# Local-attention rounds: residual and gates moved ahead of the recurrence's parts on VectorE, outputs turned in another PSUM bank

## The reference

```python
xn = _layernorm(x, axis=-1)
s = _L1_attn_ref(xn, ...)         # gated delta rule, 16 heads of 8, 256 steps in order
g = _silu(_L1_ffn_ref(xn, ...))   # two layers of local attention and a gated MLP
x = x + s * g
```

```python
S = S * jnp.exp(gt)[..., None, None]
pred = jnp.einsum('bhk,bhkv->bhv', kt, S)
dv = (vt - pred) * bt[..., None]
S = S + jnp.einsum('bhk,bhv->bhkv', kt, dv)
ot = jnp.einsum('bhk,bhkv->bhv', qt, S)
```

```python
h = shift_token(x)
q, k, v = split(h @ wqkv)
q, k = rotary_xpos(l2norm(q) * qs, l2norm(k) * ksc)
x = x + local_attention(q, k, v) @ wo
h = layernorm(shift_token(x)) * lg + lb
a, g = split(h @ w1 + b1)
x = x + (a * gelu(g)) @ w2 + b2
```

## Time and profile before

| | |
|---|---|
| median of 3 runs | 2034.4 us (2033.83 to 2039.69) |
| the profiled execution: time, span of the profile | 2048.09 us, 2046.3 us |
| mean granted clock of TensorE | 0.89 |
| busy over the span | PE 76%, DVE 74%, POOL 64%, ACT 55% |
| local rounds | from about 965 us to 2008 us of the span |
| instructions | 31347 |

### The profile page before, as it was taken

The page is one execution under the profiler, slowest core; times in us unless marked ns, Lnnn a source line. Parts: engine busy times, 40 slices in busy tenths (PEclk is TensorE's granted clock), DMA queues, the critical chain, the costliest instruction groups (busy, mean ns, idle before and its releaser), DMA issues. The chain is left out here.

```text
span 2046.3 us, 31347 instructions
## 1 busy us (share of the span) xinstructions
PE 1549.5 (76%) x10312; PEld 1086.4 (53%) x10376; DVE 1517.5 (74%) x2701; ACT 1129.3 (55%) x3167; POOL 1301.7 (64%) x1780
## 2 busy tenths in 40 slices
PE   6989898888998748731578777777778777777765
PEld 4667677677776643311355555555555555555543
DVE  2466759677686863995688888888888888888843
ACT  2356566665666733331356666666666666666643
POOL 0455446365555710554888888888888888888700
PEclk9889889998999878965689999999999999999877
DMA  2555565564756814763000000000000000000004
GB/s 84 180 179 205 172 216 193 180 207 166 244 170 207 281 50 128 234 178 112 1 15 3 17 17 17 17 6 12 17 17 17 16 6 12 17 17 17 4 3 123
DMA packets 137573, 191.97 MB, mean 94 GB/s; under 512 B 65730, under 2 KB 94788, under 8 KB 137284
## 3 DMA queue, kind: packets, MB, share of 16 engines
q0 software_dynamic: 36864, 134.76, 19.5%
q1 hardware_dynamic: 95314, 50.98, 9.1%
q10 hardware_dynamic: 5234, 4.23, 0.7%
HBM read 166.22 MB, written 23.72 MB: 93 GB/s over the span
## 5 line engine op out<-in xcount | busy, mean ns | idle before, releaser
L304 POOL DMA_INDIRECT l_rows<-in_table,l_idx x256 | 333.9, 1304 | 294.5 <-DVE l_idx L635 179.4
L437 PE MATMUL l_acc<-l_rows,ident 128*128 128x128 f32 x2048 | 310.4, 307 | 73.9 <-ACT l_rows L531 67.5
L437 PEld LDWEIGHTS l_acc<-l_rows,ident 128*128 128x128 f32 x2048 | 275.8, 214 | 109.1 <-ACT l_rows L531 100.7
L531 ACT ACTIVATE l_rows<-l_rows,l_act 128x128 f32<-128x128 f32 x1024 | 306.1, 387 | 2.1
L1315 ACT ACTIVATE lo_prob<-lo_s_ps,lo_nmx,lo_rn 128x128 f32<-128x128 f32 x512 | 226.7, 460 | 43.5 <-DVE lo_nmx L1579 41.7
L1467 POOL TENSOR_TENSOR lo_c<-lo_c 128x1024 f32<-128x1024 f32 x64 | 150.8, 2356 | 11.2 <-DVE lo_c L1569 6.8
L585 DVE TENSOR_TENSOR l_rows<-l_rows,xn_tok 128x2048 f32<-128x2048 f32 x64 | 145.9, 2279 | 8.5 <-DMA l_rows<-in_table,l_idx 8.5
L586 DVE TENSOR_REDUCE l_dot<-l_rows 128x16 f32<-128x2048 f32 x64 | 146.3, 2286 | 2.2
L403 PE MATMUL l_S<-top_out,l_AT 128*128 128x144 f32 (+3 forms) x832 | 126.4, 301 | 21.6 <-ACT l_AT L522 17.2
L522 ACT ACTIVATE l_AT<-l_log,top_bias 128x512 f32<-128x512 f32 (+1 forms) x96 | 63.9, 684 | 133.4 <-PE l_log L395 118.6
L403 PEld LDWEIGHTS l_S<-top_out,l_AT 128*128 128x128 f32 (+2 forms) x832 | 112.2, 202 | 34.5 <-ACT l_AT L522 22.6
(11 more groups left out here) (266 smaller groups left out, 3972.4 us busy)
## 6 DMA issues: line engine op xcount, KB each, us to landing
scratch_ops<-pr_ops SPq DMA_DIRECT2D x4, 1568.0 KB, 5.7
lo_de_ops<-scratch_ops SPq DMA_DIRECT2D x16, 392.0 KB, 3.7
l_rows<-in_table,l_idx POOLq DMA_INDIRECT x256
lo_de_qo<-scratch_qo SPq DMA_DIRECT2D x16, 256.0 KB, 3.9
x_tok<-in_x SPq DMA_DIRECT2D x8, 256.0 KB, 5.2
scratch_q<-pr_stage_q SPq DMA_DIRECT2D x8, 256.0 KB, 3.8
scratch_k<-pr_stage_k SPq DMA_DIRECT2D x8, 256.0 KB, 2.3
pr_Yq<-scratch_q SPq DMA_DIRECT2D x8, 256.0 KB, 3.0
```

Source lines behind the costliest of these rows:

```text
L304: pool.indirect_dma_start(rows[L][:, r % SLOTS, p, :], None, a[f"table{L}"], bass.IndirectOffsetOnAxis(ap=at[:, p:p + 1], axis=0)).then_in ...
L437: ins = pe.matmul(out, m["ident"][:], rows[L][:, r % SLOTS, p, (FAN + f) * D:(FAN + f + 1) * D], start=False, stop=(L == 5 and k == PICK - ...
L531: ins = act.activation(z, z, ACT.Copy, scale=actv[L][:, r % 2, k:k + 1])
```

## The change

Five things are changed in `local_phase`.

1. DVE's order. `residual(w)` goes ahead of `normalise(v,0)`; `query` and `o_normalise` go behind `normed(w)`; `gate(w,0)` and `gate(w,1)` go ahead of `answer`, and `gate(w,2)` between its first part (the sum over keys) and the rest.
2. `answer` is split for that in two calls, with a semaphore `o_summed` between them.
3. `maxima`: one multiplication for both groups of heads in place of two, and so one release of `exps` for both groups.
4. The turned probabilities of (w,1,1) go to o_ps in place of ft_ps, so that they wait for `keep_qk(v,1,0)` in place of `keep_qk(v,1,1)`.
5. `turn_out` uses ft_ps in place of h_ps, and `turn_out` and `keep_out` go behind the two `turn_prob(w,1,·)` and `keep_pT(w,1,·)`. The waits that guard the banks follow.

```diff
--- before.py
+++ after.py
@@ -1055,7 +1055,7 @@
...
         f2_full, f2_kept = st("qk_turned", 4), st("qk_kept", 4)
-        s_full, mx_ready, prob_ready, pn_ready = st("s_full", 2), st("mx_ready", 4), st("prob_ready", 4), st("pn_ready", 2)
+        s_full, mx_ready, prob_ready, pn_ready = st("s_full", 2), st("mx_ready", 2), st("prob_ready", 4), st("pn_ready", 2)
         pt_full, pt_kept, pv_full, o_kept = st("pt_full", 4), st("pt_kept", 4), st("pv_full", 2), st("o_kept", 2)
@@ -1063,8 +1063,8 @@
...
         S_ready, qS_read, o_ready, oss_ready, orms_ready, o_normed = (st("de_" + k) for k in ("S_ready", "qS_read", "o_ready", "oss_ready", "orms_ready", "o_normed"))
-        olog_ready = st("de_olog_ready")
-        turn_bank = lambda kind, k: o_ps if (kind, k) == ("qk", 2) else h_ps if (kind, k) == ("prob", 2) else ft_ps
+        olog_ready, o_summed = st("de_olog_ready"), st("de_o_summed")
+        turn_bank = lambda kind, k: o_ps if (kind, k) == ("qk", 2) or (kind, k) == ("prob", 3) else h_ps if (kind, k) == ("prob", 2) else ft_ps
         NH_ = NB // HB
@@ -1157,20 +1157,18 @@
...
                     pe.wait_ge(f2_kept.sem, f2_kept.after(v))
-                    if v:
-                        pe.wait_ge(pt_kept.sem, pt_kept.after(v - 1))
+                    if v - 2 >= B:
+                        pe.wait_ge(t_kept.sem, t_kept.after(v - 2 - B))
                 elif (j, e) == (0, 1):
...
                         pe.wait_ge(y2_ready.sem, y2_ready.after(v - 1))
-                    if v > B:
-                        pe.wait_ge(t_kept.sem, t_kept.after(v - 1 - B))
                 else:
                     if v + 1 < U:
-                        pe.wait_ge(f2_kept.sem, f2_kept.after(v + 1))
-                    elif v:
-                        pe.wait_ge(u_ready.sem, u_ready.after(v - 1))
+                        pe.wait_ge(f2_kept.sem, f2_kept.after(v + 1, 3))
+                    else:
+                        pe.wait_ge(o_kept.sem, o_kept.after(v, 1))
                 for k in range(NP):
@@ -1183,8 +1181,6 @@
...
                     pe.wait_ge(o_kept.sem, 2 * v + j)
-                if j and v + 1 < U:
-                    pe.wait_ge(f2_kept.sem, f2_kept.after(v + 1, 3))
                 for k in range(NP):
@@ -1201,8 +1197,6 @@
...
                     pe.wait_ge(y2_ready.sem, y2_ready.after(w - 1))
-                if w > B:
-                    pe.wait_ge(t_kept.sem, t_kept.after(w - 1 - B))
                 for k in range(NP):
@@ -1226,7 +1220,10 @@
...
                 else:
-                    pe.wait_ge(pt_kept.sem, pt_kept.after(min(w + 1, U - 1), 2 if w + 1 < U else 4))
+                    if w + 1 < U:
+                        pe.wait_ge(pt_kept.sem, pt_kept.after(w + 1, 2))
+                    else:
+                        pe.wait_ge(t_kept.sem, t_kept.after(w - 1 - B))
                 dst = (h_ps, v_ps, ft_ps)[k]
@@ -1240,8 +1237,10 @@
...
                 pe.wait_ge(y2_ready.sem, y2_ready.after(x))
+                if x + 2 < U:
+                    pe.wait_ge(f2_kept.sem, f2_kept.after(x + 2))
                 for i in (0, 1):
-                    ins = pe.transpose(h_ps[:, i * P:(i + 1) * P], y2[:, i * P:(i + 1) * P], m["ident"][:])
+                    ins = pe.transpose(ft_ps[:, i * P:(i + 1) * P], y2[:, i * P:(i + 1) * P], m["ident"][:])
                 ins.then_inc(t_full.sem, 1)
@@ -1258,11 +1257,12 @@
...
                     turn_qk(v, 1, 1)
+                if lw:
+                    turn_prob(w, 1, 0)
+                    turn_prob(w, 1, 1)
                 if lx and x >= B:
...
                 if lw:
-                    turn_prob(w, 1, 0)
-                    turn_prob(w, 1, 1)
                     weigh(w, 1)
@@ -1307,7 +1307,7 @@
...
                 for e in (0, 1):
-                    act.wait_ge(mx_ready.sem, mx_ready.after(v, 2 * j + e + 1))
+                    act.wait_ge(mx_ready.sem, mx_ready.after(v, j + 1))
                     if v:
@@ -1370,7 +1370,7 @@
...
                 act.wait_ge(t_full.sem, t_full.after(x - B))
-                act.copy(sized(m["xn_tok"][:, (x - B) * 2:(x - B) * 2 + 2, :]), h_ps[:, 0:T]).then_inc(t_kept.sem, 1)
+                act.copy(sized(m["xn_tok"][:, (x - B) * 2:(x - B) * 2 + 2, :]), ft_ps[:, 0:T]).then_inc(t_kept.sem, 1)
 
@@ -1383,11 +1383,12 @@
...
                     keep_v(u, 0)
+                if lw:
+                    keep_pT(w, 1, 0)
+                    keep_pT(w, 1, 1)
                 if lx and x >= B:
...
                 if lw:
-                    keep_pT(w, 1, 0)
-                    keep_pT(w, 1, 1)
                     keep_o(w, 1)
@@ -1508,10 +1509,13 @@
...
 
-            def answer(h):
+            def answer(h, part):
                 p, n0 = h // 2 % 2, HB * (h % 2)
                 o = o_[:, h % 2]
-                chd.link(dve.tensor_reduce(o.rearrange("p i n x -> p (i n x)"), qS[:].rearrange("p i (a k) -> p (i a) k", k=HD), AX.X, ALU.add))
+                if part == 0:
+                    dve.tensor_reduce(o.rearrange("p i n x -> p (i n x)"), qS[:].rearrange("p i (a k) -> p (i a) k", k=HD), AX.X, ALU.add).then_inc(o_summed.sem, 1)
+                    return
+                dve.wait_ge(o_summed.sem, o_summed.after(h))
                 dve.tensor_tensor(o, o, qo[:, p, 1, :, n0:n0 + HB, :], ALU.add).then_inc(o_ready.sem, 1)
@@ -1572,11 +1576,12 @@
...
                 dve.wait_ge(rn_ready.sem, rn_ready.after(v))
+                if v:
+                    dve.wait_ge(prob_ready.sem, prob_ready.after(v - 1, 2 * j + 2))
                 for e in (0, 1):
-                    if v:
-                        dve.wait_ge(prob_ready.sem, prob_ready.after(v - 1, 2 * j + e + 1))
-                    chm.link(dve.tensor_reduce(nmx[:, j, e, :], s_ps[e][:].rearrange("p (k t) -> p k t", t=P), AX.X, ALU.max, negate=True))
-                    dve.tensor_tensor(nmx[:, j, e, :], nmx[:, j, e, :], rn[:, v % 2, j, e:HEADS:2], ALU.mult).then_inc(mx_ready.sem, 1)
+                    ins = dve.tensor_reduce(nmx[:, j, e, :], s_ps[e][:].rearrange("p (k t) -> p k t", t=P), AX.X, ALU.max, negate=True)
+                chm.link(ins)
+                dve.tensor_tensor(nmx[:, j], nmx[:, j], rn[:, v % 2, j, 0:HEADS].rearrange("p (k e) -> p e k", e=2), ALU.mult).then_inc(mx_ready.sem, 1)
 
@@ -1632,29 +1637,32 @@
...
                     sums_of(u, 0)
+                if lw:
+                    residual(w)
+                if lv:
+                    normalise(v, 0)
+                if lu:
+                    parts_of(u, 1)
+                if lw:
+                    normed(w)
                 if 0 <= t - 1 < NH_:
...
                     o_normalise(t - 2)
-                if lv:
-                    normalise(v, 0)
-                if lw:
-                    residual(w)
-                if lu:
-                    parts_of(u, 1)
-                if lw:
-                    normed(w)
                 if lu:
...
                     maxima(v, 1)
-                if 0 <= t - 1 < NH_:
-                    answer(t - 1)
                 if lw:
...
                     gate(w, 1)
+                if 0 <= t - 1 < NH_:
+                    answer(t - 1, 0)
+                if lw:
                     gate(w, 2)
+                if 0 <= t - 1 < NH_:
+                    answer(t - 1, 1)
 
```

## The result

| | before | after |
|---|---|---|
| median (5 runs each, same chip) | 2034.4 us (2030.2 to 2039.8) | 2049.91 us (2044.93 to 2052.96) |
| ratio to before, 95% interval | | 1.0064 [1.0039, 1.0089] |
| profiled execution: time, span | 2048.09, 2046.3 us | 2044.93, 2043.1 us |
| instructions | 31347 | 31283 |

The change makes the kernel 0.64% slower by the ratio of the runs (0.76% by the two medians); 2007.4 us was forecast. The two profiled executions do not show it in their totals: that of before is above all its timed runs, that of after is the fastest of its own. So I compare the local rounds alone. First the page of after: the busy time of PE and POOL is what it was (1559.7 and 1305.3 us, 1549.5 and 1301.7 before), DVE's is 61 us less (1456.5 for 1517.5), and of the groups that changed, these matter here.

The account below looks back on a forecast made before the run. A loop over engines bounds the kernel: POOL 29.8 to 30.1 us, DVE-PE-ACT about 29.7. A round of 30.1 for 30.80, times 31, saves 22 us, the end 5: 2034.4 - 27 = 2007.4 us; range 1993 to 2027.

Parts of the forecast that it names:

- POOL's floor: Local rounds: the time POOL itself needs for a round when it waits for nothing, 29.77 to 30.06 us.
- POOL sets everything: Rival: collisions fall on slack and POOL never waits in the local rounds; 38 us saved, 1996 us; chance 0.12.
- The laid-out round: New DVE order laid on one old round from the end of `parts_of(u,0)`: 28.2 us without collisions, 29.7 with.
- `residual` at 4.7: DVE reaches `residual` 2.7 us after the parts and idles 2.0 us for `out_proj`, mostly time otherwise spent waiting for ACT.
- PE's wait for the gates: In front of v's projection: 1.8 us a round of PE waiting goes, as the gates come earlier.
- the end, -6.8 us for -5: Last rounds: parts end sooner behind POOL's last `rot_ready`; 5 of 6.5 us counted once.
- the bank moves: `turn_prob(w,1,1)` in o_ps and `turn_out` behind it: costed at nothing, hidden by the wait for `parts_of(u,0)`.
- From there to the end of `parts_of` is 5.5: From the start of `normalise(w,1)`, at 22.7 us, to the next parts: 5.5 us as before, making 28.2 a round.
- the collisions at 1.5 us: DVE instructions stretched by POOL's on the DVE-PE-ACT loop: 1.5 us a round, between nothing and 3.5.
- `query` moved down: `query` and `o_normalise` behind `normed` end at 11.2 us, with 2 us of cover before POOL's last `recur` write.
- The rival "slower": Gates ahead of `answer`'s rest delay `exps(w,1)` and collisions stay: 31.4 us a round, 2053 us; chance 0.09.
- The signs that I had named: Wrong if `query` delays POOL's last write, maxima or `answer` stretch over 2.6 us, or `exps(w,1)` end past 23 us.

Follow-up runs that it names:

- query early: The changed kernel with `query` alone moved back directly in front of `residual`: 2016.56 us, ratio to before 0.9889.
- after + 5 products: The changed kernel with five unused PE products a round added in front of `scores(v,0)`: 2000.57 us, ratio to before 0.9819.
- lighter POOL: Two of three halving additions in `recur` left out of four kernels, one run each: old kernel 2039.91 us, changed 2025.0, changed with five unused products 2003.97.
- Before + gates first: The old kernel with `answer` split in two and the gates put ahead as in the change: 2061.93 us, ratio to before 1.0100.
- answer first: The changed kernel with the whole of `answer` put back ahead of the three gates: 2004.44 us, ratio to before 0.9816.

## Why the prediction was wrong

**POOL's floor: right.** A round is the floor plus POOL's waits: 29.77 + 42.0 / 31 = 31.1 in after, 29.77 + 11.2 / 31 = 30.1 in query early, and 29.65 to 29.7 where it waits for nothing. This is a sum, not yet a cause: it says what a round takes once POOL's waits are known. The rival "POOL sets everything" has been reached, at 2000 us, but not by the change as made.

**The laid-out round.** The round shown above, from the end of the parts at 1556.78, by my own steps:

| step, us after the parts | forecast | after |
|---|---|---|
| exps(v,0) begin | 1.6 | 2.6 |
| residual | 4.7 | 4.9 |
| normalise(v,0) ends | 6.5 | 7.7 |
| parts_of(u,1) ends | 9.0 | 10.2 |
| query, o_normalise end | 11.2 | 12.9 |
| floors ends | 12.65 | 14.2 |
| gates 0 and 1 end | 15.8 | 17.4 |
| answer ends | 18.5 | 20.6 |
| exps(w,1) end | 22.6 | 24.6 |
| the next parts_of(u,0) ends | 28.2 | 31.3 |

With the 1.5 us of collisions that I added, the forecast's last line is 29.7.

- *Right:* `residual` at 4.7 with DVE idle in front of it; the wait in front of `normed` gone; PE's wait for the gates down to a fifth; `query` as good as never made POOL wait (once, 0.7 us); the end, -6.8 us for -5. That the bank moves cost nothing was not tried by itself.
- *The failed step, first:* "From there to the end of `parts_of` is 5.5". I took the PE work in it at the durations of before. In the round shown, `exps(w,1)` ended at 1549.28 and the parts at 1556.78, 7.5 later; in the next it is 31.3 - 24.6 = 6.7, and from 1090 to 1900 us it is 6.8 in the mean, from 5.7 to 7.5. By moving the gates ahead, the change lets PE finish its turns early and then stand still until `exps(w,1)`, and at the lower clock scores and turn take 0.9 and 0.45 us more, on the path. After + 5 products shows it: with the idle filled this step takes 5.7 in every round, 1.0 less, which by my estimate is 1.0 x 31 = 32 of the 49 us that come back; the rest goes with POOL's waits and the collisions, and was not taken apart. (With a lighter POOL, where these collisions stay, the same filling gives 30.54 - 29.88 = 0.66 us a round.) Before + gates first shows that the gates' place makes the idle. The durations of before were also no safe source: its own rows had PE at the lower clock in this round, in v's projection and the contraction, and I read them as DVE's wait of 2.37 for PE without asking why PE was slow.
- *The failed step, second:* the collisions at 1.5 us "in between". I took 1.5 us out of at most 3.5. Measured: the multiplication's mean went only from 926 to 842 ns, for 0.17 at best, twice a round, and the two products of `answer` from 1.70 to 1.39 us together, for 0.58 at best. That is 1.3 + 0.8 = 2.1 us a round. They are not random. In 10 of the 25 rounds from 1096 to 1895 us POOL waits for the parts; its addition starts 0.1 us behind them, DVE comes to the first multiplication 1.2 us after them, and it takes 1.28. In 11 POOL waits for nothing there but starts its addition 0.3 to 1.0 us behind the parts, and the multiplication takes 1.45 to 2.09. In the other 4 DVE is just ahead, and it takes 0.17. In after + 5 products DVE is so far ahead of POOL that nearly all pass, at 0.22 in the mean. So what counts is whether DVE comes level with POOL. Every kernel in which POOL waits for the parts or the roots in more than one round has a mean of 670 ns or more, every other one 291 or less; that the late parts are the cause of this was argued from the times, since they can't be taken away alone.
- *The failed step, third:* that `query` moved down leaves POOL's wait for the roots alone. I gave it 2 us of cover against POOL's last write, which was right, but `floors` stands behind it, and had none: 12.65 + 0.5 against POOL's 13.4. With everything 1.5 us late POOL waits 1.62 there. Query early shows the price, 33 us. I had also written DVE's idle of 2.0 us in front of `residual` off as a wait for ACT, where `query` fits into it.
- *The rival "slower"* had the right place, gates ahead of `answer`'s end, and 2053 us against the 2049.91 measured; but it priced only the gates' 1.2 us and the collisions, at 31.4 us a round, and not the clock. I gave it 0.09 because each of its terms had to come out at its end of the range. They are one mechanism: late exponentials make PE idle, the clock makes the parts late, late parts bring DVE level with POOL, and POOL's addition then falls on DVE's multiplication. The first two links are shown by after + 5 products, the last two are read from the traces.
- *The signs that I had named:* `exps(w,1)` ended at 24.6 in the round shown, past the 23; `query` made POOL wait once; the stretch of 2.1 us a round stayed under the 2.6. So the first sign told it, the second came in one round, the third not.

**Open.** Why answer first stays in the good pattern while 0.87 us more on PE tips it was not traced to a single instruction ahead of the first collision. A plausible reason, that its first rounds run with collisions missed by some tenths of a microsecond, was not tried. The part of the merged multiplication, about 0.7%, isn't separated from these patterns either, and the two bank moves and the place of `residual` are in every kernel derived from after and were never taken out alone.

**The best version** is the changed kernel with its idle filled: 2000.57 us, 0.9819 [0.9796, 0.9841] of before. Answer first is equal in time (0.9816) but changes pattern at small disturbances; with the five products in the changed order the rounds were nearly all alike, with `query` in either place (2000.28 us with it early).

## What to carry to other kernels

When a change lets one engine finish early, look at what TensorE does in the gap: the work behind the gap must be costed at the lower clock as a rival to the full one, and the price is paid where the path goes through it. Where two loops are within 1 us of each other, a forecast from one laid-out round holds for one phase between the engines only; ask what the later engine's wait puts on top of what, since work released by an event starts at the same place against the instructions behind that event. And an idle stretch that an order creates is the first place to put an instruction that is moved away; here that was worth 33 us.

## What the runs showed of the hardware

- A DVE instruction with two SBUF inputs that began inside POOL's 2.35 us addition ended with it, however short it is itself: 0.29 us became 2.38, 0.17 became up to 2.09. The other way round, POOL's addition took 3.23 in place of 2.35 behind a normalisation of DVE (answer first, at 1537.16). It is the exclusive lock that the Trainium skill describes (page "SBUF — State Buffer", section "SBUF: two separate sides"), and the traces agree; what I had not expected is that the collisions recur at the same place, in 21 of 25 rounds of after.
- PE's idle of 1.9 to 4.0 us was followed in many rounds, not in all, by work at the lower granted clock, 0.50, and then all of it is slow, small pieces and large: turn 1.11 for 0.66, scores 1.99 for 1.10, contraction 2.77 for 1.46, v's projection 2.04 for 1.10. Behind the same idle of 1.92 us in before, v's projection took 1.10 in some rounds and 1.63 to 1.94 in others. In after + 5 products the clock was 1.00 in the same place. I had expected such waits of an engine with slack to be free.
- Less work made a kernel slower, and idle filled with useless work made one faster: answer first 2004.44 against 2030.44 us with a lighter POOL (one run), after 2049.91 against 2000.57 us with five products more a round.
